# A fused recommendation tower: two more looked-up tables for block 2, tables and ids issued by SyncE at the start, a lookup ahead of the first transposes

## The chip, the cores and the metric

The kernel runs on one core of one Trainium2 chip, as one launch. The metric is the time of that launch on the device in microseconds (us), lower is better.

## The reference

For each of 512 samples, 32 embedding rows of 256 floats are looked up (one per table; the tables have 1000, 1250 or 12500 rows), all pairs of the 32 rows are dotted, and a three-layer network runs on the 496 products and 16 dense values. All in float32.

```python
e = stack([tbl_f[ids[:, f]] for f in range(32)], axis=1)     # [512, 32, 256]
z = dots(e)[:, i < j]                                        # [512, 496]
h = concatenate([z, dense_ctx], axis=1)                      # [512, 512]
h = maximum(h @ W_top1 + b_top1, 0)                          # [512, 512]
h = maximum(h @ W_top2 + b_top2, 0)                          # [512, 256]
y = h @ W_top3                                               # [512, 1]
```

## The kernel before

**Fetches and pairs.** The batch is cut into four blocks of 128 samples. A fetch is 128 rows of the tables, one per partition: the fields of four samples (a group). GpSimd fetches nearly all of them, one indirect DMA each (L382), into a ring of 24 buffers. Three fetches (`SINGLE`, L75) come row by row instead, 384 plain DMAs, 320 of SyncE (L359) and 64 of ACT (L778). TensorE transposes each fetch in two halves (L400); two fetches are a **pair**, and everything is ordered by pair. There are 118 fetches, 59 pairs, 115 gathers.

**Hot tables.** `HOTS = (0, 4, 4, 2)` (L33) says how many of the smallest tables are not fetched in each block. Such a table lies whole in SBUF (`hot_sb`, 1 MB, loaded in two halves). For a **unit**, one table in one block, DVE compares the block's ids with the row numbers, eight instructions that give 0/1 masks (L634); TensorE multiplies table by mask in 16 steps (L451, `look_up`, L440) into `hot_ps`; ACT copies the result to `hot_xt` (L788). There are ten units, and their steps are spread over pairs 1 to 38 (`lookups_by_pair`, L159). A unit's first step waits until the unit before it was copied (L447). With four hot tables a fetch has 28 fields per sample, and the room left in it holds rows of the block's last groups, so a block has 28 fetches for 32 groups; the last four groups ("shared", `gram_last`, L422) follow the block's last pair.

**A pair.** In the loop of TensorE (L556) pair p is transposed, then the dots of pair p-1 are taken (L415), then the pair's lookup steps, its stages of the network (`mlp_stages`, L133), and its sets. DVE copies each transposed pair out of PSUM (L317, L320, L328), makes masks, and copies half of the dots to z (L301, L308); ACT copies the looked-up fields into place (L334, L339), the other half of the dots, and issues most DMAs: tables, ids and weights by `LOAD_AT` (L178), single rows (L778), and "moves" (`move_dots`, L740), DMAs that carry pieces of z of a block to where five packed steps of h1 can use them.

**Waits that matter here.** The first move of a block waits until both engines have copied all its dots (L743, L744); the next are issued in the pairs that `MOVE_AT` (L129) names. `h1` of a block waits for its four moves (L477). `y` waits for both relus of h2 (L534, L537), one on DVE and one on ACT, each in order behind what its engine was given before. For the last block, z is multiplied in sets of 32 samples (`SET_AT`, `SUM_AT`).

**The start.** SyncE loads the ids and the row ids, then, once DVE has computed the addresses (L620), the single rows. ACT waits for the ids, loads the ids of the first hot block, waits for the first gather and loads the first table. TensorE runs 26 idle passes (L459), transposes pair 0, runs 36 more, and goes on with pair 1. DVE copies pair 0, then makes the first two masks.

## Time and profile before

| | |
|---|---|
| median of 3 runs | 241.13 us (240.97 to 241.35) |
| span of the profiled execution (its time around the span was not recorded) | 166.0 us |
| TensorE matmul busy | 147.4 us, 89% |
| TensorE weight load busy | 124.6 us, 75% |
| DVE busy | 94.0 us, 57% |
| ACT busy | 52.3 us, 31% |
| GpSimd busy | 110.5 us, 67% |
| moved by DMA | 25.25 MB, mean 152 GB/s |

The span runs from the first to the last instruction. Busy shares are averages over stages with different limits. Float32 matmuls appear twice in the records, so a lookup step is two records, and a transposed pair four records in two fetches (x4). In the timeline a row gives start, duration, engine, line and operation, then tile written and tiles read, the count of merged instructions and, in brackets, the engine's idle time before it and what ended it. "SPq" and "ACTq" are instructions of a sequencer, DMA issues among them. A chain row gives start, duration and what the chain passed through.

### The profile page before, as it was taken

To read this page: it belongs to the slowest core of one execution; us is meant where nothing else is said; L and a number is where in the kernel's file an instruction comes from. 1 tells how busy PE (TensorE), PEld (TensorE's weight loads), DVE (VectorE), ACT (ScalarE), POOL (GpSimd) and SP (SyncE) were. 2 spreads that over 40 slices of the span, in tenths; PEclk is the share of its full clock that TensorE was granted. 3 is DMA by queue.
4 is the path that set the end of the run, shared out by engine and by line. 5 is a ranking of instruction groups with operands and counts; after the bars stand their busy time and mean duration, and the time that the engine had idled before them with its cause. 6 is when DMAs were issued, how large, how long until landed. Compare 5 with 4: busy or idle time off the path is not lost.

```text
span 166.0 us, 7532 instructions
## 1 busy us (share of the span) xinstructions
PE 147.4 (89%) x2978; PEld 124.6 (75%) x2978; DVE 94.0 (57%) x299; ACT 52.3 (31%) x163; POOL 110.5 (67%) x122
## 2 busy tenths in 40 slices
PE   6897997999798793899999999998957999998894
PEld 6895985878686682788999889886846896858473
DVE  2191352567738584166953892698771566549521
ACT  0003011133113240206531551256551443618620
POOL 3777777777777777777777777777777777740000
PEclk9999999999999999699999999999996999999999
DMA  1599679886857334356776634433434433430000
GB/s 33 139 327 319 196 207 330 262 277 216 258 177 234 109 108 129 109 153 196 236 199 203 195 103 124 128 100 110 122 105 123 119 106 99 119 106 4 4 0 0
DMA packets 11218, 25.25 MB, mean 152 GB/s; under 512 B 2926, under 2 KB 4430, under 8 KB 11184
## 3 DMA queue, kind: packets, MB, share of 16 engines
q0 software_dynamic: 5520, 15.08, 30.6%
q10 hardware_dynamic: 4876, 9.25, 18.3%
q1 hardware_dynamic: 788, 0.45, 1.1%
q8 instruction: 23, 0.38, 0.9%
q14 instruction: 11, 0.09, 0.2%
HBM read 24.55 MB, written 0.00 MB: 148 GB/s over the span
## 4 chain that ended last, share of the span: by engine, by line
PE 53%; DMA 16%; POOL 15%; issue 6%; DVE 4%; ACTq 2%; ACT 2%
POOL rows L382 15%; DMA rows<-tables,idx 15%; PE hot_ps L451 14%; PE xt_ps L400 11%; PE gram_ps L415 9%; PE act_ps L481 3%; PE act_ps L526 3%; PE dve_ps L481 3%; PE dve_ps L526 2%; PE hot_ps L497 2%; DVE z L308 1%; DMA ids_sb<-ids 1%; PE dve_ps L538 1%; ACTq L349 1%; PE act_ps L507 1%
## 5 line engine op out<-in xcount | busy, mean ns | idle before, releaser
L382 POOL DMA_INDIRECT rows<-tables,idx x115 | 109.7, 954 | 36.6 <-issue 28.0
L451 PE MATMUL hot_ps<-mask,hot_sb 128*128 128x128 f32 x320 | 46.6, 291 | 3.5 <-ACT hot_xt L788 3.5
L400 PE MATMUL xt_ps<-ident,rows 128*128 128x128 f32 x228 | 38.6, 281 | 9.4 <-DMA rows<-tables,idx 9.3
L451 PEld LDWEIGHTS hot_ps<-mask,hot_sb 128*128 128x128 f32 x320 | 39.4, 194 | 5.2 <-issue 3.7
L400 PEld LDWEIGHTS xt_ps<-ident,rows 128*128 128x128 f32 x228 | 26.5, 143 | 15.3 <-DMA rows<-tables,idx 12.6
L334 ACT COPY xt<-hot_xt 128x64 f32<-128x64 f32 (+1 forms) x43 | 10.2, 236 | 59.9 <-PE gram_ps L415 56.0
L415 PEld LDWEIGHTS gram_ps<-xt 128*32 128x32 f32 x1888 | 20.8, 113 | 10.6 <-issue 9.4
L328 DVE COPY last_xt<-xt_ps 128x64 f32<-128x64 f32 (+3 forms) x44 | 10.9, 248 | 30.3 <-PE xt_ps L400 29.4
L415 PE MATMUL gram_ps<-xt 128*32 128x32 f32 x1888 | 27.5, 200 | 0.6 <-DVE xt L320 0.6
L320 DVE COPY xt<-xt_ps 128x448 f32<-128x448 f32 (+2 forms) x43 | 26.6, 620 | 0.0
L317 DVE COPY xt<-xt_ps 128x512 f32<-128x512 f32 x16 | 11.0, 690 | 21.3 <-PE xt_ps L400 21.3
L301 ACT COPY z<-gram_ps 32x128 f32<-32x128 f32 (+1 forms) x56 | 19.4, 347 | 6.8 <-PE gram_ps L415 5.6
L301 DVE COPY z<-gram_ps 32x128 f32<-32x128 f32 (+1 forms) x56 | 19.2, 343 | 0.9
L634 DVE TENSOR_SCALAR mask<-hot_ids_sb,hot_number 128x128 f32<-128x128 int32 x80 | 16.9, 302 | 0.0
L788 ACT COPY hot_xt<-hot_ps 128x256 f32<-128x256 f32 x10 | 6.2, 619 | 19.7 <-PE hot_ps L451 18.1
L459 PE MATMUL hot_ps<-ident 128*128 128x128 f32 x62 | 9.5, 327 | 1.6 <-POOL ident L372 1.6
L459 PEld LDWEIGHTS hot_ps<-ident 128*128 128x128 f32 x62 | 9.1, 174 | 1.6 <-POOL ident L372 1.6
L308 DVE COPY z<-gram_ps 32x64 f32<-32x64 f32 (+1 forms) x32 | 8.4, 263 | 1.2 <-PE gram_ps L415 0.8
L308 ACT COPY z<-gram_ps 32x64 f32<-32x64 f32 (+1 forms) x32 | 8.5, 266 | 1.7 <-PE gram_ps L415 1.3
L481 PE MATMUL act_ps<-z,w_packed_sb 128*128 128x128 f32 x48 | 7.3, 286 | 0.0
L481 PE MATMUL dve_ps<-z,w_packed_sb 128*128 128x128 f32 x48 | 7.3, 286 | 0.0
L481 PEld LDWEIGHTS act_ps<-z,w_packed_sb 128*128 128x128 f32 x48 | 6.1, 191 | 0.4 <-issue 0.2
(53 smaller groups left out, 84.4 us busy)
## 6 DMA issues: line engine op xcount, KB each, us to landing
single_rows<-tables SPq DMA_DIRECT2D x320, 1.0 KB
hot_sb<-hot_tables ACTq DMA_DIRECT2D x8, 512.0 KB, 5.2
w_sb<-w ACTq DMA_DIRECT2D x8, 256.0 KB
rows<-tables,idx POOLq DMA_INDIRECT x115
w_packed_sb<-w_packed ACTq DMA_DIRECT2D x5, 256.0 KB
single_rows<-tables ACTq DMA_DIRECT2D x64, 1.0 KB
hot_ids_sb<-hot_ids ACTq DMA_DIRECT2D x3, 256.0 KB, 4.9
w_sb<-w ACTq DMA_DIRECT2D x1, 512.0 KB, 4.0
```

Source lines behind the costliest of these rows:

```text
L301: last = copy(z_by_quad[FIELDS * jq:FIELDS * (jq + 1), q, first:end, :].rearrange("p g (h s) -> p g h s", s=FOURS), gram_ps[FIELDS * q:FIE ...
L308: last = copy(z_by_quad[FIELDS * jq:FIELDS * (jq + 1), q, first:end, lo:SLOTS], gram_ps[FIELDS * q:FIELDS * (q + 1), part % 3, 0:end - fir ...
L317: return copy(xt[:, bank, :, places].rearrange("p k l q f -> p (k l q f)"), xt_ps[:, bank, :, places].rearrange("p k l r -> p (k l r)"))
L320: return copy(xt[:, bank, :, places].rearrange("p k l q f -> p (k l) q f")[:, :, :, 0:COLD[b]], xt_ps[:, bank, :, places, 0:OWN[b]].rearra ...
L328: return copy(to[:, :, :, field:field + count].rearrange("p k s f -> p k f s"), ps)
L382: pool.indirect_dma_start(rows[:, n % RING, :], None, tables, bass.IndirectOffsetOnAxis(idx[:, fetch:fetch + 1], 0)).then_inc(rows_landed[ ...
L400: last = nc.tensor.transpose(xt_ps[:, fetch // 2 % 2, k, fetch % 2, :], x[:, P * k:P * (k + 1)], ident[:])
L415: last = nc.tensor.matmul(gram_ps[FIELDS * q:FIELDS * (q + 1), part % 3, at, :], x, x, start=(k == 0), stop=(k == CHUNKS - 1))
L451: last = nc.tensor.matmul(hot_ps[:, k, :], hot_sb[:, l, c, P * k:P * (k + 1)], mask[:, unit % MASKS, c, :], start=(c == 0), stop=(c == HOT ...
L459: nc.tensor.transpose(hot_ps[:, 0, :], ident[:], ident[:])
L481: last = nc.tensor.matmul(h1_ps[m], w1_packed_sb[:, s, P * m:P * (m + 1)], z[:, FOURS + s, samples] if s < FOURS else z_alone[:, samples], ...
L634: last = nc.vector.tensor_scalar(mask[:, unit % MASKS, c, :], hot_ids_sb[:, b, l, :], hot_number[:, c:c + 1], None, ALU.is_equal)
```

## The change

`HOTS` becomes (0, 4, 6, 2): in block 2 six tables are looked up. That makes 12 units, 26 fetches in block 2, 116 fetches in all, 58 pairs and 113 gathers; six tables now lie in SBUF, and w1 takes the room of tables 0 and 1 once they are done with. All 16 steps of unit 0 come before the first transposes; the other units take three pairs each (5, 5, 6 steps) up to pair 27, the last two four pairs each, up to pair 35. The 36 idle passes behind pair 0 are left out. SyncE, not ACT, issues the ids of the first hot block and the first two tables, between the row ids and the single rows; the other four tables come at pairs 1 to 9. DVE makes the first two masks before it copies pair 0. The network's stages of blocks 1 and 2, the moves, sets and single fetches get new pairs. `hot_xt` and `last_xt` become one tile per block.

```diff
-HOTS = (0, 4, 4, 2)
+HOTS = (0, 4, 6, 2)
-SINGLE = (43, 83, 109)
+SINGLE = (43, 81, 107)
-FIRST_IDLE_PASSES = (26, 36)
-SET_AT = {52: 0, 55: 1}
-SUM_AT = {56: 0}
+FIRST_IDLE_PASSES = 26
+SET_AT = {51: 0, 54: 1}
+SUM_AT = {55: 0}
@@ MOVE_AT
-           45: ((2, 0), (2, 1)), 46: ((2, 2), (2, 3))}
+           44: ((2, 0), (2, 1)), 45: ((2, 2), (2, 3))}
@@ mlp_stages
-    for n in range(N1):
-        at.setdefault(40 + n, []).append(("h1", 1, n // 2, n % 2, 2))
-    for m in range(2, N1):
-        at.setdefault(42 + m, []).append(("h1", 1, m, 0, 1))
+    for m in range(N1):
+        at.setdefault(39 + m, []).append(("h1", 1, m, 0, 1))
     for m in range(N2):
-        at.setdefault(47, []).append(("h2", 1, m))
-    at.setdefault(48, []).append(("y", 1))
+        at.setdefault(44, []).append(("h2", 1, m))
+    at.setdefault(45, []).append(("y", 1))
     for m in range(N1):
-        at.setdefault(48 + m, []).append(("h1", 2, m, 0, 1))
+        at.setdefault(47 + m, []).append(("h1", 2, m, 0, 1))
     for m in range(N2):
-        at.setdefault(53, []).append(("h2", 2, m))
-    at.setdefault(54, []).append(("y", 2))
+        at.setdefault(52, []).append(("h2", 2, m))
+    at.setdefault(53, []).append(("y", 2))
@@ lookups_by_pair
-    at = {}
+    at = {0: (0, 0, UNIT_STEPS)}
     pair = 1
-    for unit in range(UNITS):
+    for unit in range(1, UNITS):
         first = 0
-        for steps in (5, 5, 6) if unit in (0, 1, 2, 7) else (3, 3, 3, 3, 4) if unit > 7 else (4, 4, 4, 4):
+        for steps in (5, 5, 6) if unit < UNITS - HOTS[-1] else (4, 4, 4, 4):
@@ loads
-LOAD_AT = {1: ("table", 1, 0), 2: ("table", 1, 1), 4: ("table", 2, 0), 5: ("table", 2, 1), 6: ("ids", 1),
-           7: ("table", 3, 0), 8: ("table", 3, 1), 9: ("ids", 2),
-           **{10 + n: ("w1_packed", n) for n in range(PACKED)}, 16: ("w2",),
+FIRST_LOADS = 2
+TABLE_ORDER = tuple(sorted(FIRST_USE, key=FIRST_USE.get))[FIRST_LOADS:]
+TABLE_AT = (1, 3, 6, 8)
+LOAD_AT = {**{pair + n: ("table", l, n) for pair, l in zip(TABLE_AT, TABLE_ORDER) for n in range(2)}, 5: ("ids", 1),
+           **{10 + n: ("w1_packed", n) for n in range(PACKED)}, 15: ("ids", 2), 16: ("w2",),
            **{24 + n: ("w1", n) for n in range(SLOTS)}}
+W1_HOME = (0, 1)
+W1_HOME_FREE = 1 + max(n for n, (table, _) in enumerate(UNIT) if table in W1_HOME)
@@ SyncE
             sp.dma_start(single_sb[:], single_ids).then_inc(single_loaded, 16)
+            load_ids(sp, 0)
+            for unit in range(FIRST_LOADS):
+                for n in range(2):
+                    load_table(sp, UNIT[unit][0], n)
             sp.wait_ge(row_at_ready, 1)
@@ TensorE
-            idle(FIRST_IDLE_PASSES[0])
+            idle(FIRST_IDLE_PASSES)
+            look_up(*LOOKUP_AT[0])
             for place in range(2):
                 transpose_fetch(place)
-            idle(FIRST_IDLE_PASSES[1])
@@ DVE
-                copy_pair(pair)
                 if pair == 0:
                     make_mask(0)
                     make_mask(1)
+                copy_pair(pair)
@@ ACT
             act.wait_ge(ids_loaded, 16)
-            load_ids(0)
-            act.wait_ge(rows_landed[0], 16)
-            load_table(UNIT[0][0], 0)
-            load_table(UNIT[0][0], 1)
...
                     elif kind == "w1":
+                        act.wait_ge(looked_up, W1_HOME_FREE)
                         act.dma_start(w1_sb[:, what[0], :], w1[:, what[0], :]).then_inc(w1_loaded, 16)
```

`DOTS_AT` is computed (L109): the dots of block 2's last two parts, four and eight pieces, fall on pairs 43, 44 (4 each) and 45 (8) before, and on pair 43 (4) and pair 44 (4 and 8) after.

## Rows read from the trace of the kernel before

**Rows 1.** The page's first line.
```profile
span 166.0 us, 7532 instructions
```

**Rows 2.** The gathers: busy, mean ns, idle; then least, median, most ns, first, last start.
```profile
L382 POOL DMA_INDIRECT rows<-tables,idx x115 | 109.7, 954 | 36.6 <-issue 28.0
...
L382 POOL DMA_INDIRECT rows<-tables,idx x115: 942/946/1314, 3.4 to 146.9; - x115
```

**Rows 3.** Windows: length, busy us of five engines, granted clock, DMA share, GB/s.
```profile
10.00:35.00 25.00, 22.53 (x438) 19.64 (x436) 12.30 (x39) 3.28 (x5) 19.16 (x20) 1.00 0.86 276
35.00:60.00 25.00, 22.30 (x483) 18.27 (x482) 15.37 (x45) 7.79 (x21) 18.93 (x20) 1.00 0.66 198
...
68.00:72.00 4.00, 4.00 (x50) 3.44 (x50) 0.76 (x2) 0.24 (x1) 3.08 (x4) 0.58 0.39 109
72.00:108.36 36.36, 36.03 (x809) 32.32 (x808) 24.22 (x80) 13.44 (x39) 27.52 (x30) 1.00 0.58 171
...
125.60:129.80 4.20, 4.18 (x51) 3.95 (x52) 0.76 (x2) 0.59 (x2) 3.20 (x4) 0.59 0.38 105
```

**Rows 4.** The chain of work, at pairs 24, 28 and 36.
```profile
71.63 0.44 PE xt_ps L400 x4
72.07 0.39 PE gram_ps L415 x32
72.46 1.09 PE hot_ps L451 x8
...
79.45 1.31 PE hot_ps L451 x10
...
99.85 0.89 PE act_ps L526 x8
```

**Rows 5.** Timeline, 8 to 13 us; last, the page's DMA issues with us to landing.
```profile
8.11 4.09 PE L459 MATMUL hot_ps<-ident 128*128 128x128 f32 x36
...
8.92 3.42 DVE L634 TENSOR_SCALAR mask<-hot_ids_sb,hot_number 128x128 f32<-128x128 int32 x16
...
12.04 0.38 PE L400 MATMUL xt_ps<-ident,rows 128*128 128x128 f32 x2
...
hot_ids_sb<-hot_ids ACTq DMA_DIRECT2D x3, 256.0 KB, 4.9
```

**Rows 6.** Timeline, 62 to 68 us (pairs 20 to 22).
```profile
62.62 1.05 ACTq L753 DMA_DIRECT2D z_alone<-z  x1
...
66.32 0.61 ACT L788 COPY hot_xt<-hot_ps 128x256 f32<-128x256 f32 x1 [1.44 <-issue]
...
67.08 1.28 PE L451 MATMUL hot_ps<-mask,hot_sb 128*128 128x128 f32 x8 [3.19 <-ACT hot_xt L788]
```

**Rows 7.** SyncE's single rows (duration, first and last); timeline of pairs 40 and 41.
```profile
L349 SPq DMA_DIRECT2D single_rows<-tables x320: 227/228/507, 6.3 to 133.4; - x160
...
108.36 0.66 PE L400 MATMUL xt_ps<-ident,rows 128*128 128x128 f32 x4
...
110.33 0.38 PE L400 MATMUL xt_ps<-ident,single_rows 128*128 128x128 f32 x2
```

**Rows 8.** Timeline: block 1's last move; and the shortest landing among the DMA issues.
```profile
104.71 0.77 ACTq L753 DMA_DIRECT2D z<-z  x1
...
ids_sb<-ids SPq DMA_DIRECT2D x1, 118.0 KB, 2.2
```

**Rows 9.** Timeline: pairs 45 to 47, pair 49 and the last pair.
```profile
120.63 2.20 ACT L301 COPY z<-gram_ps 32x64 f32<-32x64 f32 x8
...
122.91 1.80 ACTq L753 DMA_DIRECT2D z_alone<-z  x2
...
125.62 0.44 PE L400 MATMUL xt_ps<-ident,rows 128*128 128x128 f32 x2 [2.44 <-DMA rows<-tables,idx]
...
132.33 0.60 PE L400 MATMUL xt_ps<-ident,rows 128*128 128x128 f32 x4
...
152.19 0.44 PE L400 MATMUL xt_ps<-ident,rows 128*128 128x128 f32 x2
```

More of the change, by code:

```diff
@@ L206, in tower_kernel @@
         mask = sb("mask", [P, MASKS, HOT_CHUNKS, BLOCK])
-        hot_xt = sb("hot_xt", [P, CHUNKS, HOT_BATCH, HOT])
+        hot_xt = [sb(f"hot_xt_{b}", [P, CHUNKS, BLOCK, HOTS[b]]) for b in range(1, BLOCKS)]
         xt = sb("xt", [P, 2, CHUNKS, 2, QUADS, FIELDS])
-        last_xt = sb("last_xt", [P, BLOCKS - 1, CHUNKS, HOT, QUADS, FIELDS])
+        last_xt = [sb(f"last_xt_{b}", [P, CHUNKS, HOTS[b], QUADS, FIELDS]) for b in range(1, BLOCKS)]
         z = sb("z", [P, SLOTS, BATCH])
         z_alone = sb("z_alone", [P, BATCH - BLOCK])
-        w1_sb = sb("w1_sb", [P, SLOTS, H1])
+        w1_sb = hot_sb[:, W1_HOME[0]:W1_HOME[-1] + 1].rearrange("p l c d -> p (l c d)").rearrange(
+            "p (s h) -> p s h", s=SLOTS)
         w1_packed_sb = sb("w1_packed_sb", [P, PACKED, H1])
@@ L326, in copy_shared @@
             field = fetch - FIRST_FETCH[b]
-            to = last_xt[:, b - 1, chunks, 0:HOTS[b]].rearrange("p k g q f -> p k (g q) f")
+            to = last_xt[b - 1][:, chunks].rearrange("p k g q f -> p k (g q) f")
             return copy(to[:, :, :, field:field + count].rearrange("p k s f -> p k f s"), ps)
         def place_hot(copy, pair):
-            s = QUADS * group_of(2 * pair) - BLOCK
             b = block_of(2 * pair)
+            s = QUADS * group_of(2 * pair) - BLOCK * b
             return copy(xt[:, pair % 2].rearrange("p k l q f -> p k (l q) f")[:, :, :, COLD[b]:FIELDS],
-                        hot_xt[:, :, s:s + 2 * QUADS, HOT - HOTS[b]:HOT])
+                        hot_xt[b - 1][:, :, s:s + 2 * QUADS])
         def place_hot_last(copy, b):
-            s = BLOCK * b - QUADS * HOTS[b]
-            return copy(last_xt[:, b - 1, :, 0:HOTS[b]].rearrange("p k g q f -> p k (g q) f")[:, :, :, COLD[b]:FIELDS],
-                        hot_xt[:, :, s:s + QUADS * HOTS[b], HOT - HOTS[b]:HOT])
+            return copy(last_xt[b - 1][:].rearrange("p k g q f -> p k (g q) f")[:, :, :, COLD[b]:FIELDS],
+                        hot_xt[b - 1][:, :, BLOCK - QUADS * HOTS[b]:BLOCK])
         def fetch_rows(engine, kind, lo, hi):
@@ L350, in fetch_rows, with load_table, load_ids @@
                                        ).then_inc(single_landed[at], 16)
+        hot_by_row = hot_tables.rearrange("l (p c) d -> l p c d", c=HOT_CHUNKS)
+        def load_table(engine, l, n):
+            half = slice(n * HOT_CHUNKS // 2, (n + 1) * HOT_CHUNKS // 2)
+            engine.dma_start(hot_sb[:, l, half, :], hot_by_row[l, :, half, :]).then_inc(hot_loaded[l][n], 16)
+        def load_ids(engine, b):
+            engine.dma_start(hot_ids_sb[:, b].rearrange("p l n -> p (l n)"),
+                             hot_ids[b:b + 1, :].to_broadcast([P, HOT * BLOCK])).then_inc(hot_ids_loaded[b], 16)
         block = ctx.enter_context(nc.Block())
@@ L424, in gram_last @@
                 for n in range(HOTS[b]):
-                    gram_group(BLOCK_GROUPS * (b + 1) - HOTS[b] + n, last_xt[:, b - 1, :, n])
+                    gram_group(BLOCK_GROUPS * (b + 1) - HOTS[b] + n, last_xt[b - 1][:, :, n])
             def wait_placed(pair):
@@ L759, in load_at @@
                     if kind == "table":
-                        load_table(*what)
+                        load_table(act, *what)
                     elif kind == "ids":
-                        load_ids(*what)
+                        load_ids(act, *what)
                     elif kind == "w1_packed":
@@ L787, in copy_looked_up @@
                 act.wait_ge(looked_up, unit + 1)
-                nc.scalar.copy(hot_xt[:, :, BLOCK * b:BLOCK * (b + 1), l], hot_ps[:, 0:CHUNKS, :]
+                nc.scalar.copy(hot_xt[b][:, :, :, l - (HOT - HOTS[b + 1])], hot_ps[:, 0:CHUNKS, :]
                                ).then_inc(hot_copied, 1)
```

8 lines of the change are left out of this document (removed).

## The prediction

> **What bounds the kernel now.** The profiled execution is known by its span alone, 166.0 us [rows 1]; the median of the three timed runs is 241.13 us, 75.1 us more. I take what lies around the span as unchanged, make every sum in the span, and put its difference on the median. I read the gathers first. GpSimd issues one every 0.946 us plus 0.3 us, without a pause, from 3.4 to 146.9 us [rows 2]: 1.25 us each, 2.5 us per pair of fetches. That is one pace. TensorE's work is the other. The windows [rows 3] show it 2.5 us idle in 10 to 35 us and 2.7 us idle in 35 to 60 us (it waits for rows), but busy in 36.0 of 36.4 us from 72 to 108.36. At the end the last pair is transposed at 152.19 [rows 9], over 4 us after the last gather was issued, right behind other TensorE work: there TensorE is late, not the rows. Two stretches run at a granted clock of 0.58 or 0.59, a mix of 2.4 and 1.2 GHz [rows 3], and each follows an idle stretch of over 2 us: 3.19 us behind ACT [rows 6], 2.44 us behind a row [rows 9].
>
> So two gathers fewer (113 for 115) can bring the end at most 2.5 us nearer by GpSimd's pace, and 4.7 us if TensorE is also never late. What counts is when TensorE reaches the last block.
>
> **Prices.** From the chain [rows 4]: a pair's transposes 0.44, its grams 0.39; four lookup steps 1.09 and five 1.31, so a step costs 0.22 and going over to such a stage 0.22 once. A step of h1 costs the same 0.22; a half of h2 0.89. A pair with n steps takes 1.05 + 0.22n us: 1.92, 2.13, 2.36 for n = 4, 5, 6.
>
> **The start: 0.** Lookup work grows from 10 units to 12, 160 to 192 steps, 7.0 us. Unit 0 (16 steps, 3.5 us) goes ahead of the first transposes. It takes the place of the 36 idle passes, 4.09 us [rows 5], which go. It needs ids, a mask and a table. SyncE issues the ids at about 1.6 us; at the median landing of 4.9 us [rows 5] they are there at 6.5, the mask (half of the 3.42 us for sixteen [rows 5]) at 8.2. The table, issued from 2.0 on, should be there at about the same time. The lookup ends near 11.8, and pair 1 starts near 12.2, where it starts now (12.04 [rows 5]). If ids or table are later the cover is the slack of the next step. The masks now stand ahead of DVE's first copy, but that copy waits for the lookup anyway.
>
> **Pairs 1 to 21: 0.** Pairs 1 to 9 have the same steps as before. Pairs 10 to 21 get 64 steps for 48: 3.5 us, against 2.7 us of idle TensorE there [rows 3]. Followed pair by pair against the arriving rows, pair 20 starts 0.3 us later, since it mostly waits for rows, and pair 22 1.0 us later. That is hidden: in pair 22 TensorE now sits 3.19 us until ACT has copied the looked-up unit at 66.32, behind its moves of z, the first at 62.62 [rows 6]. Moves, mask and last dots stand at the same pairs in the new schedule. The wait shrinks to about 2.5 us and ends at 67.3. I keep the slow clock behind it. ACT's two more copies of 0.61 us [rows 6] and DVE's two more masks of 1.7 us lie in time those engines have here. The single rows: SyncE issues one per 0.40 us from 6.3 on, the 256th near 107.8, and pair 41 used it at 110.33 without a wait [rows 7]; between the two I take 109.4. It is now wanted in pair 40. The rest of the edit I put at nothing: six fields instead of four to place in block 2 (ACT's copies of 0.2 us beside TensorE's work), the split tiles, and w1 in the room of tables 0 and 1, whose wait for unit 5 is over in pair 15 while the load stands at pair 24.
>
> **Pairs 22 to 42: +1.8 us at pair 40.** From pair 22 on both schedules hold 64 lookup steps, but the new one has them by pair 35, the old by 38. Pair 24 starts near 72.2 for 71.63 [rows 4] (one step more, half of it slow). By pair 37 five more steps have gone (1.1 us, less 0.2 for a stage saved): pair 37, before at 100.74 (pair 36, behind h2 [rows 4]) + 2.6 = 103.3, is 1.6 us later, at 104.9. So is the last move of block 1, now issued at 104.71 [rows 8]: 106.3. The bounds of its landing are 2.2 us (the shortest listed [rows 8]) and 4.9 (ids, [rows 5]); the moved pieces are small, I take 2.6: 108.9. The first h1 of block 1 stands at pair 39 instead of 40. Pairs 37 and 38 carry no lookups now (1.0 and 1.3 us), so TensorE is there at 104.9 + 2.3 + 0.9 = 108.1 and **waits 0.8 us**. With its five steps pair 40 starts at 110.2 for 108.36 [rows 7], and the single row is there. Pairs 40, 41, 42 (five h1 steps each): 6.4 us and 0.2 for two stages that end late, so pair 43 starts at 116.8. Its grams include six shared groups, 1.3 us, then pair 44 at 119.1.
>
> **Pairs 44 to 47: the new wait.** In pair 44 two parts of z are copied together: 12 pieces of 0.275 us (eight take 2.20 [rows 9]), 3.3 us on each of DVE and ACT, behind 1.8 us of placing and the dots of pair 43 on ACT. Behind them on ACT stand two moves (1.80), and only then h2's relu (0.37). Counted from pair 44's start: 1.8 + 3.3 + 0.1 + 1.8 + 0.4 = 7.4 us, and y, in pair 45, waits for that relu. Pair 46 thus starts at +7.7 instead of +4.2. The other two moves (0.77 each, as the one of [rows 8]) follow, the last is issued near +8.5 and lands near +10.8; h1 of block 2 in pair 47 waits for it (about 1.3 us). Pair 48 starts at +12.1, 131.2. In the old order the same work of the last block starts with pair 49, at 132.33 [rows 9]. That is **1.1 us earlier**; TensorE's idle parts may bring a slow stretch again (before: one at 125.6 to 129.8 [rows 3]), but it would lie mostly beside the wait, 0.1 us. All behind it is the same work, and its rows arrive 2.5 us earlier than now. Sum: 0 + 0 - 1.1 + 0.1 = -1.0 us, **240.1 us**. Its own bounds, 0.4 to 0.5 us either way for the landing, a slow stretch and the late stages, give 239.0 to 241.0.
>
> **A rule against the pace of the gathers.** The gathers' mean of 0.954 us is 0.012 above their least [rows 2], 1.4 us in all 115, the first one's 0.37 included, while DVE made 80 mask instructions of 0.21 us (3.42 for sixteen [rows 5]); if each held one gather up for its length, 16.8 us would be missing. So 16 more cost at most 0.2 us. The Trainium skill, SBUF — State Buffer, in its part on engine contention (the port pair that VectorE and GpSimd share), says that a VectorE instruction in a two-port mode keeps GpSimd from writing descriptors for its full length. By the skill's rule 16 more mask instructions could cost 16 x 0.21 = 3.4 us of GpSimd and the last gather would come 0.9 us later than now; the row speaks against it, and the sum stays with the row.
>
> **Rivals.** (1) *Rows set the end.* The waits of pairs 39, 45 and 47 don't come, since ACT runs ahead of what I count, or the shorter wait in pair 22 leaves the clock at 2.4 GHz (0.42 of 4 us, 1.7 us [rows 3], are won there). Then the last transposes follow the last gather: 152.2 - 4.7 = 147.5, time 236.4; halfway there 238.3. For it: without waits TensorE's work from pair 43 on is 2.3, 7.3 for pairs 44 to 47, and 19.9 behind them (132.33 to 152.19 [rows 9]), 29.5 us, which from 116.8 ends at 146.3. Against it: ACT's order is written down. Chance 0.17.
> (2) *The start eats it.* The new kernel loads 2.1 MB more before pair 10, where the DMA engines are already busy for 0.86 of the time, at 276 GB/s [rows 3]. Rows then land later, TensorE reaches pair 20 some 1 us later than I count, and all behind moves with it: 241.1, no change. The Trainium skill, DMA: Bandwidth & Descriptors, in its part on queues and rings, says that each engine takes turns between the queues it has work for; if so, tables on SyncE's queue and on ACT's leave the gathers a third of the turns. For it: that share; against: from pair 10 on TensorE can make good about 0.3 us a pair (2.5 less 2.2). Chance 0.18.
> (3) *Slower: SyncE is late with the single rows.* Five issues of 2.5 MB stand ahead of them. If they hold SyncE or its queue until the data has moved (2.5 MB at 276 GB/s is 9 us, from 1.6 to 10.7, for a first row issued at 6.3 [rows 7]), the 256th row lands 4.4 us later, 113.8, instead of being 0.8 us early at pair 40. It decides from 0.8 us on, one for one, and beyond 1.8 us the change loses: with all 4.4 us by 3.6 - 1.0 = 2.6, 243.7; with half of them by 0.4, 241.5. For it: pair 40 wants it now, one pair sooner. Against: ACT issues a DMA in 0.8 to 0.9 us [rows 8, 9] with others in flight. Chance 0.2.
>
> **How the numbers follow.** 0.2% is 0.48 us, about what the measurement can tell from none. Forecast 0.45, of which three quarters are faster by more; with rival 1 and small parts of the others that makes faster 0.53. Same: a fifth of the forecast and most of rival 2, 0.21. Slower 0.26. The likeliest is 240.1; the range 237.3 to 242.1 leaves out the best end of rival 1 and the worse half of rival 3.
>
> **What would show it.** Pair 1 starts near 12.2 and TensorE waits for ACT again near 64 to 67 us; then three waits: h1 of block 1 on the moves near 108, y of block 1 on ACT's relu near 122 to 126, h1 of block 2 on the moves near 128. The last transposes start near 151, the last gather is issued near 144.4. I am wrong if the transposes of pair 40 wait for single_rows, if TensorE waits for rows in the last 20 us of gathers, or if gathers take over 1 us each.

## The result and the profile after: slower by 1.6%

The changed kernel takes 244.4 us (median of 4 runs, 243.85 to 246.03) where the kernel before takes 241.05 us (4 runs, 240.95 to 241.35): a ratio of 1.0163, 95% interval 1.0119 to 1.0206. I had forecast 240.1 us, in a range of 237.3 to 242.1, with a chance of 0.53 for faster. Both the size and the sign are wrong. A median here is that of all runs, but a ratio leaves out the runs that lay more than 1.5% above the fastest of their kernel on that chip, so it can differ from the ratio of the two medians.

The page of the changed kernel, its first line, parts 1 and 4 and the gathers and lookups of part 5:

```profile
span 242.1 us, 7605 instructions
PE 174.6 (72%) x3002; PEld 148.0 (61%) x3002; DVE 96.3 (40%) x313; ACT 53.2 (22%) x164; POOL 108.8 (45%) x120
...
PE 59%; another core or an unknown queue 17%; issue 11%; ACT 5%; DVE 3%; ACTq 3%; DMA 2%; SPq 0%; DVEq 0%
...
L399 POOL DMA_INDIRECT rows<-tables,idx x113 | 108.0, 956 | 89.8 <-PE xt_ps L417 58.1
...
L468 PE MATMUL hot_ps<-mask,hot_sb 128*128 128x128 f32 x384 | 57.5, 302 | 13.8 <-ACT hot_xt L790 6.3
```

Against [rows 1] the surprise is the first line. The span is 242.1 us, not some 165, and this execution's time was 243.93: only 1.8 us lie around a span, not 75.1. GpSimd now stands still for 89.8 us, 58.1 of them because TensorE has not emptied a ring buffer, where [rows 2] has 36.6 us, the 0.3 us between gathers and little more. So the traced execution of before and the timed ones are not of the same sort.

The runs below show why: the same program takes some 166 us on some chips and some 241 us on others, the trace of before came from the first kind and the times from the second. I call them the 166 us chips and the 241 us chips, and first measured both kernels on both.

### The profile page after: what moved, and what is told of

The parts are those of the page before. It is cut to its first block, busy times and chain, and to the rows that moved or that the text cites. A ratio compares the mean times of both kernels' runs of the same rounds, so it can differ in the third digit from the quotient of the medians.

```text
span 242.1 us, 7605 instructions
## 1 busy us (share of the span) xinstructions
PE 174.6 (72%) x3002; PEld 148.0 (61%) x3002; DVE 96.3 (40%) x313; ACT 53.2 (22%) x164; POOL 108.8 (45%) x120
## 3 DMA queue, kind: packets, MB, share of 16 engines
q10 hardware_dynamic: 4732, 9.25, 12.5%
## 4 chain that ended last, share of the span: by engine, by line
PE 59%; another core or an unknown queue 17%; issue 11%; ACT 5%; DVE 3%; ACTq 3%; DMA 2%; SPq 0%; DVEq 0%
PE hot_ps L468 20%; PE gram_ps L432 14%; PE xt_ps L417 11%; PE act_ps L498 4%; PE dve_ps L498 3%; DMA hot_ids_sb<-hot_ids 2%; ACT z L305 2%; PE hot_ps L514 1%; DVE mask L651 1%; PE act_ps L543 1%; ACTq L352 1%; ACT hot_xt L790 1%; ACT z L312 1%; PE dve_ps L555 1%
## 5 line engine op out<-in xcount | busy, mean ns | idle before, releaser
L399 POOL DMA_INDIRECT rows<-tables,idx x113 | 108.0, 956 | 89.8 <-PE xt_ps L417 58.1
L432 PE MATMUL gram_ps<-xt 128*32 128x32 f32 x1856 | 41.4, 207 | 40.0 <-DVE xt L321 22.8
L468 PE MATMUL hot_ps<-mask,hot_sb 128*128 128x128 f32 x384 | 57.5, 302 | 13.8 <-ACT hot_xt L790 6.3
L432 PEld LDWEIGHTS gram_ps<-xt 128*32 128x32 f32 x1856 | 30.6, 115 | 55.2 <-issue 30.6
L468 PEld LDWEIGHTS hot_ps<-mask,hot_sb 128*128 128x128 f32 x384 | 50.3, 208 | 16.1 <-issue 15.0
L417 PE MATMUL xt_ps<-ident,rows 128*128 128x128 f32 x224 | 37.5, 292 | 0.2 <-issue 0.2
L332 DVE COPY last_xt<-xt_ps 128x64 f32<-128x64 f32 (+4 forms) x43 | 11.4, 264 | 57.7 <-PE xt_ps L417 54.7
L338 ACT COPY xt<-hot_xt 128x32 f32<-128x32 f32 (+2 forms) x42 | 10.3, 244 | 95.9 <-remote 61.2
L324 DVE COPY xt<-xt_ps 128x448 f32<-128x448 f32 (+3 forms) x42 | 25.7, 611 | 0.0
L651 DVE TENSOR_SCALAR mask<-hot_ids_sb,hot_number 128x128 f32<-128x128 int32 x96 | 20.0, 301 | 2.3 <-DMA hot_ids_sb<-hot_ids 2.3
L432 PE MATMUL gram_ps<-last_xt 128*32 128x32 f32 x192 | 4.7, 225 | 3.8 <-issue 3.8
L498 PEld LDWEIGHTS dve_ps<-z,w_packed_sb 128*128 128x128 f32 x48 | 6.9, 216 | 0.2
```

The source lines that it names most:

```text
L324: return copy(xt[:, bank, :, places].rearrange("p k l q f -> p (k l) q f")[:, :, :, 0:COLD[b]], xt_ps[:, bank, :, places, 0:OWN[b]].rearra ...
L332: return copy(to[:, :, :, field:field + count].rearrange("p k s f -> p k f s"), ps)
L338: return copy(xt[:, pair % 2].rearrange("p k l q f -> p k (l q) f")[:, :, :, COLD[b]:FIELDS], hot_xt[b - 1][:, :, s:s + 2 * QUADS])
L399: pool.indirect_dma_start(rows[:, n % RING, :], None, tables, bass.IndirectOffsetOnAxis(idx[:, fetch:fetch + 1], 0)).then_inc(rows_landed[ ...
L417: last = nc.tensor.transpose(xt_ps[:, fetch // 2 % 2, k, fetch % 2, :], x[:, P * k:P * (k + 1)], ident[:])
L432: last = nc.tensor.matmul(gram_ps[FIELDS * q:FIELDS * (q + 1), part % 3, at, :], x, x, start=(k == 0), stop=(k == CHUNKS - 1))
```

## The same two kernels on both kinds of chip

Six runs were kernels left unchanged; the sixth, r16, stands further down. Expected and measured:

**r1_before_again** (no edit). 

> The kernel before, unchanged, profiled again. Theory A (the profile read before the prediction, span 166.0 us, is of an execution unlike the timed ones): the span is about 239 us, 1.8 us under the timed 241, with TensorE's pairs held up by stalls like those of the changed kernel, and GpSimd no longer gathering without a pause. Theory B (the profile is typical and 75 us lie outside the span; the changed kernel's 242.1 us span, 1.8 us under its time, is new): span 166 us again, time 241 us.

It took 166.63 us (8 runs; the before of the same chip 167.29), its span was 165.4. That is neither theory: on this chip the time itself is 75 us less.

**r3_after_again** (no edit). 

> The changed kernel, unchanged, on a chip where the kernel before takes 167 us. My prediction's sum, made in a span of 166.0 us, stands to be tested here: span 165.0 us (1.0 us less), with waits of TensorE for block 1's moves near 108, for ACT's relu before y near 122 to 126, and for block 2's moves near 128, last transposes near 151. If instead the change costs what the first measurement said (ratio 1.016), the span is about 168.7. If the late start alone decides (pair 1 near 14.8 and pair 2 later than before), the waits for rows go and the end is 2 to 3 us late.

On a 241 us chip, so the sum in a span of 166 us was not tested here: 244.19 us (6 runs), before 241.02 (11 runs), ratio 1.0173 [1.0109, 1.0237].

**r5_before_same_chip** and **r6_after_same_chip** (no edit), on one 166 us chip. 

> The kernel before, unchanged, beside the two below on one chip. On a chip of the first kind (before near 167 us) its trace repeats the one read: span near 166. On a chip of the second kind (before near 241) my theory is that the 74 us more are stalls in which semaphore updates of TensorE reach the other engines late and SyncE's single-row instructions take 0.7 us each, everywhere in the first 200 us, while GpSimd gathers, as in the changed kernel: pair 22 then starts after 100 us instead of 63, and the last 13 us are as on the other kind. Rival: the same pace of pairs, with 74 us lost in one place.

> The changed kernel beside it. On a chip of the first kind my prediction's sum is tested: span 1.0 us under that of before, and its three new waits (pairs 39, 45, 47). The run with the start on ACT gave 166.3 there with the last pair at 152.5, so the rival says 0 to +1 us. On the second kind it repeats 244 and a ratio of 1.016 to 1.017.

Before 166.29 us (11 runs), changed 169.3 (6 runs, 168.03 to 170.22): ratio 1.0185 [1.0144, 1.0226]. **The change costs 3.0 us on one kind and 3.2 to 4.0 on the other** (the last in r16, below). So the loss is not made by the slow kind of chip, though, as shown below, its parts differ.

**r11_before_beside** (no edit) gave the trace of before that was missing, on a 241 us chip. 

> The kernel before, unchanged, for a trace from the same chip as the three others. On a chip where it takes about 166 us it shows pair 49 starting near 130 and one slow stretch of the clock, behind pair 22. On a chip where it takes about 241 us: if the 75 us belong to the chip and not to the order of the work, TensorE idles about 20 us beside semaphore updates that come late near the start and grams are spaced out up to 200 us, as in the changed kernel; if only the changed kernel stalls so, this trace has no such stretch and its 241 us need another cause.

It took 240.74 us (2 runs; the traced one 238.73, span 236.9). Its 75 us belong to the chip: TensorE is held up in the same place in both kernels. The timeline of TensorE and two other engines, first the changed kernel, then before (r11), behind the first transposes:

```profile
14.38 1.04 PE L417 MATMUL xt_ps<-ident,rows 128*128 128x128 f32 x8
...
32.65 0.95 POOL L399 DMA_INDIRECT rows<-tables,idx  x1 [0.30 <-issue]
37.42 0.61 ACT L790 COPY hot_xt<-hot_ps 128x256 f32<-128x256 f32 x1 [30.61 <-remote]
37.51 1.29 DVE L321 COPY xt<-xt_ps 128x512 f32<-128x512 f32 x2 [27.36 <-remote]
...
38.25 0.66 PE L432 MATMUL gram_ps<-xt 128*32 128x32 f32 x32 [22.83 <-DVE xt L321]
```

```profile
23.40 0.21 PE L415 MATMUL gram_ps<-xt 128*32 128x32 f32 x1 [1.90 <-issue]
24.79 0.21 PE L415 MATMUL gram_ps<-xt 128*32 128x32 f32 x1 [1.18 <-issue]
26.89 0.21 PE L415 MATMUL gram_ps<-xt 128*32 128x32 f32 x1 [1.89 <-issue]
29.00 0.21 PE L415 MATMUL gram_ps<-xt 128*32 128x32 f32 x1 [1.90 <-issue]
31.79 0.21 PE L415 MATMUL gram_ps<-xt 128*32 128x32 f32 x1 [2.58 <-issue]
```

In the changed kernel the copies that wait for TensorE's work from 14.38 on start only at 37.4 (ACT) and 37.5 (DVE), while GpSimd gathers on up to 33 us; in before the grams crawl, one in 1.4, 2.1 or 2.8 us, multiples of 0.70. Either way pair 2 starts at 41.1 and at 42.9 us, on the 166 us chips at 16.8 and 15.5. This stands in the kernel before too, which has no tables on SyncE's queue, so the new start is not its cause. And behind it TensorE stumbles on up to some 200 us, for as long as gathers are issued. One pair of before, r11, then the same work in r5:

```profile
62.78 0.27 PE L415 MATMUL gram_ps<-xt 128*32 128x32 f32 x8
63.48 0.51 PE L415 MATMUL gram_ps<-xt 128*32 128x32 f32 x24 [0.44 <-issue]
63.92 1.38 PE L451 MATMUL hot_ps<-mask,hot_sb 128*128 128x128 f32 x10
```

```profile
51.74 0.44 PE L400 MATMUL xt_ps<-ident,rows 128*128 128x128 f32 x2 [0.28 <-DMA rows<-tables,idx]
52.11 0.46 PE L415 MATMUL gram_ps<-xt 128*32 128x32 f32 x32
```

On the 241 us chip the 32 grams are cut by a gap of 0.44 us that nothing in the profile releases; on the other they run through, and TensorE waits for a row instead. The waits of TensorE up to pair 20 or so, as us in total, times and longest: a line each of r5 and r6 (both 10 to 60 us), then two of r11 (42 to 105):

```profile
PE xt_ps L400 <- DMA rows<-tables,idx: 5.2, 7, 1.2
```

```profile
PE xt_ps L417 <- DMA rows<-tables,idx: 1.5, 3, 0.8
```

```profile
PE gram_ps L415 <- issue: 11.0, 25, 0.5
PE hot_ps L451 <- ACT hot_xt L788: 1.9, 2, 1.4
```

This is what decides between the kinds. On a 166 us chip TensorE has 5.2 us of waiting for rows, the room I put the new lookups in, and 1.5 us of it is left. On a 241 us chip no wait for rows is listed in this stretch, in r11 or in the changed kernel (its result's trace, 41 to 105 us): TensorE's own gapped work sets the pace, so new lookups find no such room.

## Where the time goes

Starts of pairs in four executions, in us (the text takes differences before rounding). The last block's work starts with pair 49 before and pair 48 after; the pair with the shared groups is 44 before and 43 after.

| start of | r5 before | r6 after | r11 before | after (result) |
|---|---|---|---|---|
| pair 10 | 35.8 | 35.1 | 68.7 | 69.1 |
| pair 20 | 58.9 | 59.5 | 101.8 | 104.3 |
| pair 44 / 43 | 115.8 | 116.4 | 184.0 | 186.7 |
| pair 49 / 48 | 129.9 | 132.3 | 203.3 | 208.4 |
| last pair | 149.8 | 152.1 | 223.1 | 228.2 |
| span | 164.1 | 165.9 | 236.9 | 242.1 |

In these pairs of traces two places hold it all. From pair 10 to the start of pair 20 the changed kernel has 13 of its lookup steps more (53 for 40): 1.4 us on the 166 us chip, where 0.7 us had been gained before pair 10, and 2.2 us on the 241 us chip. From the pair with the shared groups to the last block it takes 15.9 us for 14.1, and 21.7 for 19.2: **1.8 and 2.5 us**. What lies ahead of pair 10, from pair 20 to 43 and behind pair 48 differs by less than 0.8 us in each.

One trace is one execution, and r11 and the result come from two chips, so here are the same stretches in all traces of the 241 us chips (r12's left out, the slowest of its ten runs), in us:

| stretch | old order: r11, r14, r15, r18 | new order: result, r3, r4, r8, r9, r10, r13, r16, r17 |
|---|---|---|
| pair 10 to 20 | 33.0 to 35.1 | 35.3 to 37.1 |
| pair 20 to the shared groups | 82.2 to 84.5 | 81.9 to 83.2 |
| from there to the last block | 19.2 to 19.7 | 21.4 to 21.7 (result, r3, r10, r16, where this stretch is as in the change) |

The first and the last row part the two orders, the middle one doesn't. The first row's means are 33.7 and 36.0: 2.3 us for 13 steps, 2.9 us by my price. On the 166 us chips the last row can't be read so: there before took 14.1 us in r5, but 16.1 in r1 and 16.6 in the trace of [rows 9], each with a wait of 2.5 us for a row and a granted clock of 0.50 behind it (r5: a wait of 1.2 us, clock 1.00), and the changed kernel 15.9 in r6.

The second place, ScalarE and TensorE in the timeline of the changed kernel, r6:

```profile
118.91 0.66 PE L417 MATMUL xt_ps<-ident,rows 128*128 128x128 f32 x4
...
121.41 3.32 ACT L305 COPY z<-gram_ps 32x64 f32<-32x64 f32 x12
...
124.40 0.38 PE L555 MATMUL dve_ps<-h,vec_sb 128*1 128x128 f32 x2 [0.79 <-DVE h L676]
124.81 2.10 ACTq L754 DMA_DIRECT2D z_alone<-z  x2
126.96 0.37 ACT L820 ACTIVATE h<-act_ps,vec_sb 128x128 f32<-128x128 f32 x1 [2.24 <-issue]
...
127.38 0.38 PE L555 MATMUL dve_ps<-h,vec_sb 128*1 128x128 f32 x2 [2.60 <-ACT h L820]
127.69 0.90 PE L417 MATMUL xt_ps<-ident,rows 128*128 128x128 f32 x4
...
130.78 1.42 PE L498 MATMUL act_ps<-z,w_packed_sb 128*128 128x128 f32 x8
```

Twelve pieces of dots, then two moves, then h2's relu: y, and with it all of TensorE, waits 2.60 us in pair 45. Behind that wait the granted clock was 0.50 (1.2 GHz) from 128.0 to 131.4 us, so pairs 46 and 47 ran slowly, and h1 of block 2, the last line, waited for nothing. On the 241 us chips y's wait is 3.6 to 3.9 us. Before, in r5, the moves come a pair later beside TensorE's work, h2 follows them, and y waits for nobody:

```profile
124.80 1.16 PE L526 MATMUL act_ps<-h,w_sb 128*128 128x128 f32 x8
...
125.05 1.61 ACTq L753 DMA_DIRECT2D z<-z  x2
...
127.09 0.37 ACT L818 ACTIVATE h<-act_ps,vec_sb 128x128 f32<-128x128 f32 x1
...
127.83 0.60 PE L538 MATMUL dve_ps<-h,vec_sb 128*1 128x128 f32 x4
```

## Experiments on the start

**r2_act_start, r7_act_start_same_chip**: the first ids and tables issued by ScalarE.

```diff
-            load_ids(sp, 0)
-            for unit in range(FIRST_LOADS):
-                for n in range(2):
-                    load_table(sp, UNIT[unit][0], n)
...
             act.wait_ge(ids_loaded, 16)
+            load_ids(act, 0)
+            for unit in range(FIRST_LOADS):
+                for n in range(2):
+                    load_table(act, UNIT[unit][0], n)
```

> The changed kernel with the ids of the first hot block and the first two tables issued by ACT again, behind its wait for the ids, instead of by SyncE. If the 22 us stall at 15.4 to 37.4 us comes from SyncE's queue (its single rows behind 2.5 MB of its own), it goes or shrinks to a few us and the time falls towards 222 us. If it comes from something else that all engines share (rival), it stays at some 20 us, perhaps elsewhere, and the time stays within 3 us of 244.

> The changed kernel with the first ids and tables issued by ACT. On a chip of the first kind: within 1 us of the changed kernel. On the second: if the 22 us stall of 15.4 to 37.4 us is of SyncE's queue, with 2.5 MB ahead of the single rows, it goes and the time is some 20 us less than 244; if it is of the second kind of chip as such, whatever is in that queue, the stall stays and the time is within 3 us of 244.

r2: 168.56 and 172.61 us in two runs, before 167.29, which tells nothing. r7, beside r6: 168.95 us (4 runs), 1.0156 [1.0105, 1.0206] of before, where the changed kernel has 1.0185: no difference that can be told. SyncE's issues are not the loss on this kind of chip. Both runs fell on 166 us chips, so what they were to say of the 22 us stall is said by r11 alone.

**r10_idle38**: `FIRST_IDLE_PASSES = 26` becomes 38. 

> The changed kernel with 38 idle passes ahead of the first lookup for 26. TensorE idled 2.2 us before that lookup, waiting for VectorE's first mask, and then ran it at half the clock, 3.5 us of slow clock. If the start counts, the lookup's 16 steps take 3.5 us for 5.4, pair 1 starts 1.5 to 2 us earlier and the end comes 1 to 2 us earlier. If the start is absorbed by the waits of pairs 10 to 22, the end stays within 0.5 us. If 12 more idle passes last beyond the mask, the lookup starts later by what they overrun, under 0.5 us.

244.45 us (4 runs), 1.0144 [1.0026, 1.0261]. The lookup did run at the full clock, and pair 0 started at 12.5 us, but pair 1 at 15.5 and pair 2 at 41.1 us, as in the result: the gain is absorbed by the stall.

**r15_before_new_start**: the kernel before with the new start alone.

```diff
-    at = {}
-    pair = 1
-    for unit in range(UNITS):
+    at = {0: (0, 0, UNIT_STEPS)}
+    pair = 4
+    for unit in range(1, UNITS):
...
+            load_ids(sp, 0)
+            for unit in range(2):
+                for n in range(2):
+                    load_table(sp, UNIT[unit][0], n)
...
-            idle(FIRST_IDLE_PASSES[0])
+            idle(FIRST_IDLE_PASSES)
+            look_up(*LOOKUP_AT[0])
...
-                copy_pair(pair)
                 if pair == 0:
                     make_mask(0)
                     make_mask(1)
+                copy_pair(pair)
```

> The kernel before with the new start alone: SyncE loads the first ids and two tables, unit 0 (16 steps) is looked up ahead of the first transposes, the two masks stand ahead of VectorE's first copy, the 36 idle passes go; pairs 1 to 3 have no steps, from pair 4 on all is as before, 4 tables in block 2, 115 gathers. If the start costs nothing, within 0.5 us of the kernel before. If the start carries the loss (TensorE 1.5 to 2.3 us later at pair 1, its rows held up by 2.5 MB of tables), 1 to 3 us over the kernel before. If lookups in pairs 1 to 3 were in the way of the rows, up to 1 us under it.

241.85 us (4 runs) where before had 243.77 on that chip (25 runs, 240.85 to 245.54): 0.9889 [0.9805, 0.9972]. That would be a gain; r18 below, with 12 runs, has 0.9991. **The start costs nothing that can be told**, on this kind of chip, and the gain is not confirmed.

## Experiments on the order in pairs 44 to 48

**r4_y_late**: h2 and y of block 1 two pairs later.

```diff
-        at.setdefault(44, []).append(("h2", 1, m))
-    at.setdefault(45, []).append(("y", 1))
+        at.setdefault(46, []).append(("h2", 1, m))
+    at.setdefault(47, []).append(("y", 1))
```

 

> The changed kernel with h2 of block 1 at pair 46 and its y at pair 47 (instead of 44 and 45), as far behind block 2's end as in the kernel before. If y waits for ACT's relu behind two parts of dots and two moves (my prediction's new wait, 3.5 us), that wait goes and pair 46 starts 3 us earlier; the wait of h1 of block 2 for the moves stays, so the end moves by 0 to -1.5 us against the changed kernel. If the wait isn't there (rival), the time is the same within 0.3 us.

244.04 us (4 runs), 1.0133 [1.0020, 1.0246], beside r3's 1.0173: no gain that can be told from four runs. Pair 46 started at 197.9 us for 202.8 in r3, but pair 48 at 207.6 for 207.8. That is not the whole of it: this execution reached pair 43 at 187.8 us, r3 at 186.3, with nothing changed up to there, and from pair 43 to 48 it took 19.8 us for r3's 21.4. In the stretch that was edited it is as fast as the old order; by its times that isn't shown.

**r8_stages_later**: all stages of blocks 1 and 2 and the sets at the old pairs (the lines of the sets are left out).

```diff
-        at.setdefault(39 + m, []).append(("h1", 1, m, 0, 1))
+        at.setdefault(40 + m, []).append(("h1", 1, m, 0, 1))
...
-        at.setdefault(44, []).append(("h2", 1, m))
-    at.setdefault(45, []).append(("y", 1))
+        at.setdefault(47, []).append(("h2", 1, m))
+    at.setdefault(48, []).append(("y", 1))
...
-        at.setdefault(47 + m, []).append(("h1", 2, m, 0, 1))
+        at.setdefault(48 + m, []).append(("h1", 2, m, 0, 1))
```

> The changed kernel with the layer stages of blocks 1 and 2 and the last sets' sums at the pairs where the old order had them: h1 of block 1 in pairs 40 to 43, h2 in 47, y in 48, h1 of block 2 in 48 to 51, h2 in 53, y in 54. Lookups, loads, gathers, dots and moves stay. If the loss is TensorE's waits at pairs 45 to 47 (y of block 1 on ScalarE's relu, 2.6 us, then h1 of block 2), pairs 44 to 46 now run on with rows that are there, the waits fall away and it is 1.5 to 3.5 us under the changed kernel, so at or under the kernel before. If TensorE's work as a whole is what sets the end, the end stays within 0.5 us of the changed kernel, 3 us over the kernel before.

247.9 us (4 runs), 1.0267 [1.0171, 1.0364]: slower still, which neither theory had. ScalarE's moves now stood ahead of its placing of pair 47, and the grams waited for that:

```profile
203.42 2.10 ACTq L754 DMA_DIRECT2D z_alone<-z  x2
...
205.62 0.22 ACT L338 COPY xt<-hot_xt 128x32 f32<-128x32 f32 x1 [2.29 <-issue]
...
205.99 0.66 PE L432 MATMUL gram_ps<-xt 128*32 128x32 f32 x32 [2.28 <-ACT xt L338]
```

And with block 1's y and one more stage of h1 left for pair 48 and later, pairs 48 to 57 took 21.7 us, 19.8 in the changed kernel. So moving the stages can also move TensorE's wait for ScalarE to another instruction.

**r9_no_moves2**: no moves of block 2 and no wait for them; its packed pieces of z are left stale, that part is not computed.

```diff
-           44: ((2, 0), (2, 1)), 45: ((2, 2), (2, 3))}
+           }
...
+                    if b < 2:
-                    pe.wait_ge(moved[b], 16 * MOVES)
+                        pe.wait_ge(moved[b], 16 * MOVES)
```

> The changed kernel without the four moves of block 2's dots that ScalarE issues in pairs 44 and 45, and without h1's wait for them; it leaves out that part of the computation (the packed pieces of block 2 keep what they had). If ScalarE's order (dots, two moves of 0.8 to 0.9 us, only then h2's relu) makes y of block 1 wait, the wait of 2.6 us in pair 45 shrinks to 0.5 to 1 us, h1 of block 2 doesn't wait in pair 47, and the time is 2 to 3 us under the changed kernel. If something else holds the end (rows, or TensorE's work), it gains under 0.5 us.

241.2 us (10 runs) beside before's 242.09 (13 runs), 0.9966 [0.9911, 1.0021]; the wait ahead of y is 1.8 us, h1 of block 2 doesn't wait, and pairs 43 to 47 take 18.6 us. On the same chip r10, the changed kernel with more idle passes at its start, has 244.45 us, 1.0144 and 21.6 us: 3.3 us more by the medians, 4.3 by the ratios, 3.0 in these pairs. Against the changed kernel on other chips of the kind (244.2 to 245.1 us, ratios of 1.0161 to 1.0173) it is 3.0 to 3.9 us by the medians and 4.7 by the ratios. That is as much as the first theory expected or more.

**r12_sp_moves, r17_sp_moves_beside**: the same four moves, all computed, issued by SyncE, which is idle then.

```diff
+            for n in range(MOVES):
+                move_dots(sp, 2, n)
...
-           44: ((2, 0), (2, 1)), 45: ((2, 2), (2, 3))}
+           }
```

> The changed kernel with the four moves of block 2's dots issued by SyncE, idle since its last single row, in place of ScalarE. All is computed. ScalarE then has the 12 pieces of dots and right behind them h2's relu; the two moves of 2.1 us between them are gone. If that order is what costs, y of block 1 waits about 2 us less, and what is left of h1's wait for the landing is small: 1.5 to 3 us under the changed kernel, at the time of the kernel before (within 1 us of it). If the moves cost by their transfer (landing) and not by ScalarE's issue, it gains under 0.5 us.

> The changed kernel with block 2's four moves on SyncE, beside the changed kernel on one chip. If ScalarE's row of dots, moves and relu carries the loss, 1.5 to 3 us under the changed kernel; if the gain of r12 (1.006 of before, against 1.016 to 1.018 in other series) was the chip's spread, under 0.5 us.

r12: 244.71 us (10 runs) beside before's 243.77 (25 runs), 1.0060 [1.0009, 1.0111]. r17 has the changed kernel beside it: **r16_after_beside** 

> The changed kernel, unchanged, on the same chip as the next two, so that they can be set against it and not only against the kernel before. From the two earlier series: 1.015 to 1.019 of the kernel before.

r16: 245.11 us (6 runs), 1.0161 [1.0105, 1.0217]. r17: 243.04 us (11 runs), 1.0102 [1.0059, 1.0144]. The medians differ by 2.1 us; the intervals of the two ratios to before just overlap, and r12 and r9 point the same way. The timeline of r16, then of r17, around the wait:

```profile
201.27 2.10 ACTq L754 DMA_DIRECT2D z_alone<-z  x2
203.42 0.37 ACT L820 ACTIVATE h<-act_ps,vec_sb 128x128 f32<-128x128 f32 x1 [2.23 <-issue]
...
203.84 0.59 PE L555 MATMUL dve_ps<-h,vec_sb 128*1 128x128 f32 x2 [3.93 <-ACT h L820]
```

```profile
198.73 3.29 ACT L304 COPY z<-gram_ps 32x64 f32<-32x64 f32 x12
...
202.05 0.37 ACT L821 ACTIVATE h<-act_ps,vec_sb 128x128 f32<-128x128 f32 x1
202.10 1.92 SPq L377 DMA_DIRECT2D z_alone<-z  x2
...
202.47 0.38 PE L571 MATMUL dve_ps<-h,vec_sb 128*1 128x128 f32 x2 [1.78 <-ACT h L821]
```

3.93 us become 1.78, and from pair 43 to pair 48 r17 takes 19.5 us for 21.7 in r16: the second place of the table is gone (19.2 to 19.7 in the old order). What is left of the loss, 1.0%, lies ahead of pair 43.

**r13_sp_moves_dots**: r12, and the second last part's dots a pair sooner (`ready + 1` for `ready + 2`), so that 8 pieces stand ahead of the relu for 12. 

> The kernel of r12 with the two pieces of the part of z before block 2's last one copied a pair sooner, in pairs 42 and 43, so that pair 44 has 8 pieces of dots (2.2 us) for 12 (3.3 us). If ScalarE's queue in pair 44 is the bound, y's wait shrinks by another 1 us and the end comes 0.5 to 1 us sooner than with r12. If the sooner pieces push the placing of pair 43 back, or another work holds the end, no gain or a loss of up to 1 us.

245.13 us (10 runs), 1.0072 [1.0025, 1.0119]: no gain over r12. The queue was shorter: the relu follows the 8 pieces at once, and pair 46 starts 6.8 us behind pair 44 for 8.2 in r17. But y's wait stayed at 1.9 us, since its first half, behind DVE's own 8 pieces, came sooner as well; then h1 of block 2 waited 1.4 us for SyncE's moves to land (1.0 in r17) and ran at a granted clock of 0.50, 2.05 us for 1.13. Pair 48 starts 13.3 us behind pair 44, for 13.5.

**r14_before_sp_moves**: the kernel before with these moves on SyncE. 

> The kernel before with the same four moves issued by SyncE. There h2 of block 1 stands a pair behind the moves and y another, and the trace showed at most 0.4 us of TensorE's wait on that chain: a gain of 0 to 0.7 us. Should it gain 2 us or more, the moves cost in the old order as well, and they don't explain the change's loss.

242.33 us (10 runs), 0.9981 [0.9929, 1.0032]: the old order did not pay for them, as its trace says.

**r18_start_and_sp**: r14 and r15 in one. 

> The kernel before with the new start and with block 2's four moves on SyncE: four tables in block 2, 115 gathers. The moves alone changed nothing that can be told (0.998). If the new start gains what r15 showed (0.989, from four runs), 1.5 to 3 us under the kernel before. If that was spread and the start costs nothing, within 1 us of it; if TensorE's later pair 1 costs, 1 to 2 us over it.

240.38 us (12 runs) against 241.09 (22 runs): 0.9991 [0.9948, 1.0033]. No version tried here is shown to beat the kernel before.

r18 also parts the loss. It shares the start and SyncE's moves with r17 and the chip with r16 and r17, and lacks only the rest of the change: the two units, the two gathers fewer, the new order. r17's 243.04 us are 2.7 more than r18's 240.38. Their traces are as long from the shared groups to the last block (19.5 us each) and differ from pair 10 to 20: 37.1 us for 33.0. So of the 4.0 us between r16 and before on this chip, ScalarE's moves are 2.1 and the rest of the change 2.7, less 0.7 between r18 and before, which can't be told from none.

## Why the prediction was wrong, step by step

Three steps failed. The room for the new lookups was read from a trace of another kind of chip than the timed one. The last block's start was set against that of one execution that a late row had delayed, which turned a loss into a gain. And ScalarE's queue in pairs 44 and 45 is 1.0 us longer than I summed.

**"I take what lies around the span as unchanged."** Failed, and first. A difference of 75.1 us between a span and its program's time is no overhead: every run here has 1.8 to 2.3 us. It said that the trace and the times were of different executions, so that room read from the one might not be there in the other.

**"Pairs 1 to 21: 0."** Right where I read it: pair 20 at 59.5 us in r6, 0.6 later than in r5 (I had 0.3), pair 22 1.4 later (1.0), the wait for ACT 2.8 us (2.5). Wrong where it was timed, and this is the first term that failed: the 2.7 us of idle TensorE that were to hide the work were not there. Without waits for rows, 13 of the 16 steps, 2.9 us by my price, cost 2.2 us between pairs 10 and 20 against r11 (2.3 by the means of all traces), and pair 20 starts 2.5 us later.

**The start: 0.** Right as a sum, wrong in its times. The mask was there at 8.55 us for 8.2, but TensorE had idled 2.20 us, and from 8.5 to 11.9 us its granted clock was 0.50 (1.2 GHz):

```profile
6.65 3.33 DVE L651 TENSOR_SCALAR mask<-hot_ids_sb,hot_number 128x128 f32<-128x128 int32 x16 [2.06 <-DMA hot_ids_sb<-hot_ids]
...
8.55 5.43 PE L468 MATMUL hot_ps<-mask,hot_sb 128*128 128x128 f32 x32 [2.20 <-DVE mask L651]
```

5.43 us for 3.5, and pair 1 at 14.3 us for 12.2. I had seen such stretches behind idle times of 2.4 and 3.2 us and not looked for one here. By pair 10 nothing is left of it (35.1 us for 35.8 before).

**Pairs 22 to 42.** Right on the 166 us chip: pair 37 at 104.6 us (I had 104.9), pair 40 at 110.0 (110.2), pair 43 at 116.4 (116.8), pair 44 at 118.9 (119.1). The half clock behind the wait in pair 22 didn't come, so pair 24 started at 71.2 us for the 72.2 I had, and from there to pair 37 TensorE took 33.4 us for my 32.7: that the later pairs agree so well is in part luck. h1 of block 1 waited for its moves in pair 39 as said, 0.82 us for 0.8, and the single rows were there in pair 40:

```profile
108.80 1.13 PE L498 MATMUL act_ps<-z,w_packed_sb 128*128 128x128 f32 x8 [0.82 <-DMA z<-z]
...
110.21 0.38 PE L417 MATMUL xt_ps<-ident,single_rows 128*128 128x128 f32 x2
```

**"Pairs 44 to 47: the new wait."** The wait of y for ScalarE was right, and its term was too small. The relu ended 8.4 us behind pair 44's start for 7.4: the dots began at +2.5 for +1.8, and the two moves took 2.10 us for 1.80. Pair 46 started at +8.8 for +7.7. The wait of h1 in pair 47, 1.3 us, didn't come; in its place stood the slow stretch that I had put at 0.1 us, since it would lie beside the wait: from pair 46 to 48 TensorE took 4.6 us for my 4.4, without a wait, at a granted clock of 0.50 (1.2 GHz) from 128.0 to 131.4 us. Two errors of a like size cancel here. Pair 48 started at 132.3 us for 131.2.

**"That is 1.1 us earlier."** Here the sign was lost. I set 131.2 against 132.33, the last block's start in the one trace of before. But in that execution TensorE had waited 2.44 us for a late row [rows 9] and then run at a granted clock of 0.59 [rows 3]. r1 shows the same (131.7), r5 does not (129.9): an event of some executions (two of three traced on such chips), not the order's price. On the 241 us chips no trace of the old order has a wait for a row there, and there the new order costs about 2 us in these pairs where I had a gain. Against r5 my own sum would have said +1.3 us, a loss; measured are +2.3. I knew of the wait, since I listed the row, and did not ask what the sum would be without it.

**The rivals.** (1) Rows set the end: no; the last gather is issued at 144.06 us in r6 (I had 144.4) and the last pair starts at 152.1. (2) The start eats it: no; r18 has 0.9991, and gathers land in a median of 3.7 us for 3.6 in r5, so what the Trainium skill, DMA: Bandwidth & Descriptors, says on queues and rings did not show in the landings. (3) SyncE late: no; its last row is issued at 134.1 us in r6, and pair 40 doesn't wait for single_rows. I had one rival on the slower side and it was of SyncE, when the wait that I had found myself, with a longer ScalarE queue or a fairer baseline, was the nearest.

**The rule on the shared port.** I kept with the row against the Trainium skill, SBUF — State Buffer, its part on engine contention. Beside the 3.33 us of masks above, two gathers of r6 took 1.01 and 1.07 us for 0.95; the mean of all is 952 ns for 954 [rows 2]. Sixteen more masks cost GpSimd nothing that shows. By the page's rule, if these masks ran in a two-port mode, my estimate was 3.4 us; which mode they ran in no run shows.

**The sum, as it should have been.** On the 166 us chips: 0.6 us up to pair 43, 1.8 in pairs 43 to 47, and 0.5 given back behind them, 1.8 by the spans; the medians say 3.0, so the traced r6, the fastest of its six, and r5 understate it by about 1 us, which I can't place. On the 241 us chips: 2.5 us by pair 20, 0.2 to pair 43, 2.5 to pair 48, 5.2 by these two spans, 4.0 by the medians of the last series (245.11 less 241.09; r11's 238.73 us is near the lowest time of its chip). That ScalarE's moves carry some 2 us of it is shown by r17 and r9, and that most of the rest comes with the rest of the change, ahead of pair 43, by r17 beside r18. That it is the lookups' work on a TensorE without slack is read from the traces: no run took the lookups out by themselves, and ScalarE has a part in it (in r16 TensorE waits 3.2 us for its copies of looked-up units between 69 and 106 us, in r18 1.4 us between 68 and 102).

## What to carry to other kernels

Before a sum is made, set the profile's own span against the timed runs; where they differ by more than a few us, the slack that the profile shows is not the slack that is timed. And when a forecast is a difference of two points in one execution, ask whether the earlier or the later one was delayed by an accident of that execution. An engine that issues DMAs between its computing stands still for them: four moves in ScalarE's order cost 2 us that an idle SyncE gives back, but only where another engine waits for what stands behind them; in the old order (r14) they cost nothing that can be told.

## What was not expected of the hardware

The kernel before has spans of 164 to 167 us on two chips and of 237 to 244 on four, with DMA work of the same size (25.25 MB, 11218 packets for 11219). On the slower kind SyncE's row instructions, 228 ns in the median on both, now and then take 0.70 us and more:

```profile
L352 SPq DMA_DIRECT2D single_rows<-tables x320: 227/228/529, 6.8 to 134.1; - x160
```

```profile
L349 SPq DMA_DIRECT2D single_rows<-tables x320: 2/228/809, 6.3 to 168.2; - x160
```

(minimum, median and maximum in ns, r6 and then r11), and TensorE's grams stand apart by multiples of 0.70 us. It ends about where the gathers end (in r11 the last gather is issued at 196.4 us, the last such gap is at 197.3): pairs 48 to 57 take 19.8 us on either kind. What in the chip does it stays open; no run here varied anything that could tell.
